# Spreading the experts' combination over the first attention units, splitting the mask matmuls, and moving one inverse root to GpSimd

## What is computed

```python
x = x + global_latent_attn(rmsnorm(x, norm1_w), ...)   # causal, 16 heads of 8, 4 key/value heads
x = x + local_gqa_attn(rmsnorm(x, norm2_w), ...)       # window of 32 keys
...
expert_inputs = jnp.einsum('bnd,bnec->becd', token_inputs, dispatch)
h = jax.nn.gelu(jnp.einsum('becd,edh->bech', expert_inputs, W1))
expert_outputs = jnp.einsum('bech,ehd->becd', h, W2)
output = jnp.einsum('becd,bnec->bnd', expert_outputs, combine)
...
x = x + attn(xn) + ffn(xn)
```

## Time and profile before

| | us |
|---|---|
| median of 3 runs | 802.06 |
| lowest and highest | 799.94, 804.38 |
| the profiled execution | 804.5 |
| its span in the trace | 802.7 |
| experts of layer 1, first `up` to last `e_out` | 555.0 to 589.3 |
| combination on PE | 589.4 to 598.5 |
| attention, first mask matmul to the end | 599.4 to 802.7 |

### The profile page before, as it was taken

How to read it: one execution, slowest core, us unless ns; L and a number is a source line. 1 busy time by engine, 2 the same in 40 slices (tenths; PEclk the granted TensorE clock), 3 DMA queues, 4 the chain that set the end, 5 groups by cost and what they waited for, 6 DMA issues and landing times.

```text
span 802.7 us, 13340 instructions
## 1 busy us (share of the span) xinstructions
PE 676.3 (84%) x4403; PEld 491.5 (61%) x4403; DVE 586.0 (73%) x863; ACT 535.1 (67%) x1021; POOL 416.6 (52%) x362
## 2 busy tenths in 40 slices
PE   5899968888988887988969876698888888888986
PEld 3588837666676675865857666687673343444433
DVE  7435679999989999899989897983435435655532
ACT  4364577868768686787787885735637657766563
POOL 6301078998989989889998897730000000000000
PEclk8799999999899997999979978899999999999998
DMA  5324558577595785755858768800200000000000
GB/s 168 106 80 132 162 159 214 169 203 208 182 243 165 174 236 176 205 185 168 233 166 203 193 178 229 249 1 27 79 2 0 1 1 2 1 2 1 14 14 27
DMA packets 80963, 99.54 MB, mean 124 GB/s; under 512 B 32496, under 2 KB 37624, under 8 KB 80896
## 3 DMA queue, kind: packets, MB, share of 16 engines
q1 hardware_dynamic: 80896, 98.70, 43.4%
HBM read 96.05 MB, written 2.72 MB: 123 GB/s over the span
## 4 chain that ended last, share of the span: by engine, by line
PE 42%; DVE 17%; ACT 15%; issue 14%; POOL 8%; DMA 3%; DVEq 0%; POOLq 0%; SPq 0%; ACTq 0%
POOL drive L648 5%; DVE ps L1161 4%; PE ps L1772 4%; PE ps L2064 3%; DVE moe L1161 3%; PE ps L1823 3%; PE ps L1838 3%; POOL hc L656 3%; PE ps L2033 3%; ACT ps L851 2%; PE ps L2041 2%; PE ps L1907 2%; PE ps L1702 2%; DVE hc L1169 2%; PE ps L2071 2%
## 5 line engine op out<-in xcount | busy, mean ns | idle before, releaser
L648 POOL TENSOR_TENSOR drive<-dtu,b_sb 128x512 f32<-128x512 f32 x160 | 202.6, 1274 | 6.0 <-DMA b_sb<-bc_rows 5.9
L656 POOL TENSOR_TENSOR hc<-moe,c_sb 128x512 f32<-128x512 f32 x128 | 162.9, 1273 | 26.6 <-DVE moe L1161 26.5
L1161 DVE TENSOR_TENSOR_SCAN moe<-ps,drive 128x512 f32<-128x512 f32 x128 | 153.5, 1199 | 0.2 <-POOL hc L656 0.2
L1772 PE MATMUL ps<-ident,hc 128*128 128x128 f32 x1024 | 147.5, 293 | 0.6 <-POOL hc L656 0.6
L1772 PEld LDWEIGHTS ps<-ident,hc 128*128 128x128 f32 x1024 | 129.8, 153 | 25.8 <-issue 24.8
L1161 DVE TENSOR_TENSOR_SCAN ps<-decay_sb,ps 128x512 f32<-128x512 f32 x96 | 117.3, 1222 | 29.0 <-ACT ps L851 14.4
L1068 ACT ACTIVATE probs<-ps 128x1024 f32<-128x1024 f32 (+1 forms) x96 | 87.6, 914 | 67.4 <-PE ps L2041 57.0
L851 ACT ACTIVATE ps<-dt,negA 128x510 f32<-128x510 f32 x160 | 105.7, 676 | 14.9 <-DVE moe L1161 11.0
L661 POOL TENSOR_TENSOR stat<-stat,halfc 128x4 f32<-128x4 f32 x7 | 7.0, 1007 | 193.4 <-DVE stat L1426 193.4
L1169 DVE TENSOR_TENSOR hc<-ps,c_sb 128x512 f32<-128x512 f32 x128 | 85.3, 666 | 0.0
L1750 PE MATMUL ps<-xm,dtuT 128*128 128x128 f32 x384 | 59.6, 305 | 14.8 <-DMA xm<-spot_rows 8.4
(11 more groups left out here) (281 smaller groups left out, 1231.0 us busy)
## 6 DMA issues: line engine op xcount, KB each, us to landing
b_sb<-bc_rows SPq DMA_DIRECT2D x128, 256.0 KB, 4.1
c_sb<-bc_rows SPq DMA_DIRECT2D x128, 256.0 KB, 4.5
xm<-spot_rows SPq DMA_DIRECT2D x48, 256.0 KB, 3.8
wbuf<-in_pack SPq DMA_DIRECT2D x16, 514.0 KB, 3.4
wbuf<-in_pack SPq DMA_DIRECT2D x8, 512.0 KB, 3.5
x_sb<-in_x SPq DMA_DIRECT2D x4, 256.0 KB, 3.6
spot_rows<-c_sb SPq DMA_DIRECT2D x4, 256.0 KB, 4.6
out<-x_sb SPq DMA_DIRECT2D x4, 256.0 KB, 2.3
```

The lines of the kernel that those rows point to most:

```text
L648: pool.tensor_tensor(drive_of(N, half), dtu[:, N // STATES % 2, half], b_sb[:, N % B_RING], ALU.mult) \
L656: pool.tensor_tensor(hc[:, 2 * (N % DEEP) + half], h_of(q), c_sb[:, N % C_RING], ALU.mult).then_inc(sem["hc_pooled"], 1)
L1161: dve.tensor_tensor_scan(h_of(q)[:, turn], decay_bank(q)[:, turn], source[:, turn], 0.0, ALU.mult, ALU.add).then_inc(sem["scan_done"], 1)
L1772: last = pe.matmul(ps[:, Y_BANK + half, block], hc[:, 2 * (N % DEEP) + half, block], ident[:], start=False, stop=True, is_transpose=True, ...
```

## The change

- The combination becomes eight events through `PREP_BANK`: `et` k (four transposes and ACT's copy to `eo`) and `cb` k (eight matmuls, and four DVE instructions that multiply by the gate and add into `x_sb`). They sit in slots 5, 6, 16, 17 (`et`) and 7, 8, 18, 20 (`cb`). The separate stage after the experts is gone.
- The events of group 1 go one slot later (`T` three), `L1` now follows unit 0.
- In the readers' list T, L, O1 and `et` now stand ahead of the slot's exponentials.
- `FILL_AT` is written out: K0 and `sqr0` with expert 1, `inv0` with 5, `split0` and turn(0,0) with 6, `rms1`, turn(0,1) and turn(0,2) with 7.
- The inverse root of group 0 is one GpSimd power of 128x80 instead of Ln and Exp on ACT.
- Each mask matmul becomes two of 64x64, so that the two heads of a unit use four different quarters of the array; two halves of the masks are loaded a second time, swapped, by two more DMAs.
- The first two `average` wait for the last expert's `e_out`.

PE's list after begins `unit0 T1 L1 unit1 Q1 unit2 turn1,0 unit3 average0 copy0 turn1,1 K1 unit4 sqr1 et0 unit5 average1 back0 turn1,2 inv1 et1 unit6 split1 rms2 cb0 unit7 average2 copy1 cb1 unit8 turn2,0 unit9 ...`, and later has `... et2 unit16 inv2 et3 unit17 average7 back4 turn3,2 split2 cb2 unit18 O10 rms3 unit19 average8 copy5 cb3 unit20 turn4,0 O20 unit21 ...`. The readers' list has `... et1 unit6 back0 inv1 unit7 average2 split1 rms2 cb0 unit8 copy1 cb1 turn2,0 unit9 ...`.

```diff
@@ -238,16 +238,19 @@
             if name != "L" or G < GROUPS // 2:
-                put(12 * G + at, name, G)
+                put(12 * G + at + (G == 1 and name not in ("rms", "O1", "O2")) + 2 * ((name, G) == ("T", 1)), name, G)
+    for k, (turned_at, added_at) in enumerate(((5, 7), (6, 8), (16, 18), (17, 20))):
+        put(turned_at, "et", k)
+        put(added_at, "cb", k)
     order, readers = [], []
...
             unit.append(("average", at // 2 - 1))
-        first = [ev for ev in here if ev[0] == "turn"]
+        first = [ev for ev in here if ev[0] in ("turn", "T", "L", "O1", "et")]
         order += here + unit
-        readers += first + unit + [ev for ev in here if ev[0] != "turn"]
+        readers += first + unit + [ev for ev in here if ev not in first]
     return order, readers
@@ -256,16 +259,18 @@
 BLOCKS = ((0, 0), (1, 1), (0, 1))
+HALF_ROWS = (slice(0, P // 2), slice(P // 2, P))
 UNITS1 = 2 * SEQS * len(BLOCKS) * KV // 2
...
 FILL = AT_READERS[:AT_READERS.index(("unit", 0))]
-assert set(FILL) == set(AT_ORDER[:len(FILL)])
-AT_ORDER, AT_READERS = AT_ORDER[len(FILL):], AT_READERS[len(FILL):]
-LATER = FILL[4:]
-FILL_AT = {e: LATER[2 * (e - 1):2 * e if e < EXPERTS - 1 else None] for e in range(1, EXPERTS)}
+EARLY_AT = AT_ORDER[:AT_ORDER.index(("unit", 0))]
+AT_ORDER, AT_READERS = AT_ORDER[len(EARLY_AT):], AT_READERS[len(FILL):]
+FILL_AT = {1: [("K", 0), ("sqr", 0)], 2: [], 3: [], 4: [], 5: [("inv", 0)], 6: [("split", 0), ("turn", 0, 0)],
+           7: [("rms", 1), ("turn", 0, 1), ("turn", 0, 2)]}
+FILL = FILL[:4] + [ev for e in range(1, EXPERTS) for ev in FILL_AT[e]]
 TURN = {ev: n for n, ev in enumerate(ev for ev in FILL + AT_ORDER if ev[0] == "turn")}
-PREP = {ev: n for n, ev in enumerate(ev for ev in FILL + AT_ORDER if ev[0] in ("T", "L", "Q", "K", "O1", "O2"))}
+PREP = {ev: n for n, ev in enumerate(ev for ev in FILL + AT_ORDER if ev[0] in ("T", "L", "Q", "K", "O1", "O2", "et", "cb"))}
 
@@ -418,7 +423,7 @@
         rope_k = sb("rope_k", [P, 2, 2, GT * KV * HD])
-        masks = sb("masks", [P, 3, P], F16)
+        masks = sb("masks", [P, 5, P], F16)
         ident16 = sb("ident16", [P, P], F16)
@@ -572,7 +577,9 @@
                                   (w_kvu, "w_kvu"), (w_kv, "w_kv"), (w_o, "w_o"), (w_g, "w_g"), (tri, "tri")):
-                    sp.dma_start(dst[:], a[name]).then_inc(sem["l1_weights_loaded"], 16)
+                    sp.dma_start(masks[:, 0:3] if name == "masks" else dst[:], a[name]).then_inc(sem["l1_weights_loaded"], 16)
+                for rows, other in (HALF_ROWS, HALF_ROWS[::-1]):
+                    sp.dma_start(masks[rows, 3:5], a["masks"][other, 0:2]).then_inc(sem["l1_weights_loaded"], 16)
                 sp.dma_start(iota32[:], a["iota32"].partition_broadcast(P)).then_inc(sem["l1_weights_loaded"], 16)
@@ -744,6 +751,10 @@
                     rms_pow(ev[1])
+                elif ev == ("sqr", 0):
+                    pool.wait_ge(sem["qk_var"], 1)
+                    pool.tensor_tensor(norm[:, 3], norm[:, 1], halfc[:, 0:1].broadcast_to([P, QH + KH]), ALU.pow) \
+                        .then_inc(sem["qk_inv"], 1)
 
@@ -991,10 +1002,10 @@
                     act.activation(qk_sqr[:], qk[:, r].rearrange("p h d -> p (h d)"), ACT.Square).then_inc(sem["qk_sq"], 1)
-                elif kind == "inv":
+                elif kind == "inv" and G:
                     act.wait_ge(sem["qk_var"], G + 1)
                     act.activation(norm[:, 2], norm[:, 1], ACT.Ln).then_inc(sem["qk_ln"], 1)
-                    act.wait_ge(sem["qk_ln"], G + 1)
+                    act.wait_ge(sem["qk_ln"], G)
                     after(act, "qk_normed", G)
@@ -1005,6 +1016,11 @@
                         .then_inc(sem["qk_hi"], 1)
+                elif kind == "et":
+                    act.wait_ge(sem["prep_ready"], PREP[ev] + 1)
+                    act.wait_ge(sem["d_turned"], 8)
+                    act.activation(eo[:, 2 * G:2 * G + 2].rearrange("p b s d -> p (b s d)"), ps[:, PREP_BANK], ACT.Copy) \
+                        .then_inc(sem["prep_free"], 1)
                 elif kind == "O1":
@@ -1050,12 +1066,6 @@
 
-            for k in range(4):
-                act.wait_ge(sem["e_turn"], k + 1)
-                act.wait_ge(sem["d_turned"], 8)
-                act.activation(eo[:, 2 * k:2 * k + 2].rearrange("p b s d -> p (b s d)"), ps[:, k], ACT.Copy) \
-                    .then_inc(sem["e_turned"], 1)
-
             def exps(U):
@@ -1387,7 +1397,7 @@
                 n = ts.stop - ts.start
-                dve.wait_ge(sem["l1_weights_loaded"], 13 * 16)
+                dve.wait_ge(sem["l1_weights_loaded"], 15 * 16)
                 link(dve.tensor_scalar(route[:, 2, ts], route[:, 0, ts], 0.0, None, ALU.is_equal))
@@ -1513,7 +1523,7 @@
                     dve.wait_ge(sem["qk_sum"], G + 1)
-                    after(dve, "qk_ln", G)
+                    after(dve, "qk_ln", G - 1)
                     dve.tensor_scalar(norm[:, 1], norm[:, 0], 1.0 / HD, RMS_EPS, ALU.mult, ALU.add).then_inc(sem["qk_var"], 1)
@@ -1525,6 +1535,13 @@
                                       ALU.subtract).then_inc(sem["qk_split"], 1)
+                elif kind == "cb":
+                    dve.wait_ge(sem["prep_ready"], PREP[ev] + 1)
+                    for t in range(4):
+                        row = x_sb[:, 4 * G + t]
+                        last = dve.scalar_tensor_tensor(row, ps[:, PREP_BANK, t * D:(t + 1) * D], rstat[:, 3, 4 * G + t:4 * G + t + 1],
+                                                        row, ALU.mult, ALU.add)
+                    last.then_inc(sem["prep_free"], 1)
                 elif kind == "O2":
@@ -1571,15 +1588,6 @@
                 fill(e + 1)
-            for k in range(4):
-                dve.wait_ge(sem["e_comb"], k + 1)
-                rows = slice(4 * k, 4 * k + 4)
-                dve.tensor_tensor(sq[:, rows], ps[:, 4 + k % 2].rearrange("p (t d) -> p t d", d=D),
-                                  rstat[:, 3, rows].unsqueeze(2).broadcast_to([P, 4, D]), ALU.mult) \
-                    .then_inc(sem["e_added"], 1)
-            dve.wait_ge(sem["e_added"], 4)
-            dve.tensor_tensor(x_sb[:], x_sb[:], sq[:], ALU.add).then_inc(sem["x1_ready"], 1)
-
             def head_out(n):
@@ -1637,7 +1645,7 @@
 
-                pe.wait_ge(sem["l1_weights_loaded"], 13 * 16)
+                pe.wait_ge(sem["l1_weights_loaded"], 15 * 16)
                 if part == 0:
@@ -1892,7 +1900,17 @@
                     pe.wait_ge(sem["heads_done"], GT * (G + 1))
-                if kind == "L":
+                if kind == "et":
+                    pe.wait_ge(sem["e_out"], EXPERTS)
+                    for n in range(4):
+                        last = pe.transpose(bank[:, n * P:(n + 1) * P],
+                                            xe[:, 2 * G + n // 2, 4 * (n % 2):4 * (n % 2) + 4].rearrange("p e c -> p (e c)"), ident[:])
+                elif kind == "cb":
+                    for t in range(4):
+                        for two in range(2):
+                            last = pe.matmul(bank[:, t * D:(t + 1) * D], slotT[:, two, 4 * G + t], eo[:, 2 * G + t // 2, two],
+                                             start=(two == 0), stop=(two == 1))
+                elif kind == "L":
                     last = pe.matmul(ps[0:LAT, PREP_BANK], w_kvd[:], xmT[:, k * GT * P:(k + 1) * GT * P], start=True, stop=True)
@@ -2000,20 +2018,6 @@
             down(EXPERTS - 1)
-            pe.wait_ge(sem["e_out"], EXPERTS)
-            for k in range(4):
-                for n, (b, s) in enumerate(((2 * k, 0), (2 * k, 1), (2 * k + 1, 0), (2 * k + 1, 1))):
-                    last = pe.transpose(ps[:, k, n * P:(n + 1) * P], xe[:, b, 4 * s:4 * s + 4].rearrange("p e c -> p (e c)"), ident[:])
-                last.then_inc(sem["e_turn"], 1)
-            for k in range(4):
-                pe.wait_ge(sem["e_turned"], k + 1)
-                after(pe, "e_added", k - 1)
-                for t in range(4):
-                    for s in range(2):
-                        last = pe.matmul(ps[:, 4 + k % 2, t * D:(t + 1) * D], slotT[:, s, 4 * k + t], eo[:, 2 * k + t // 2, s],
-                                         start=(s == 0), stop=(s == 1))
-                last.then_inc(sem["e_comb"], 1)
-
             def scores(U):
@@ -2030,8 +2034,11 @@
                     elif kt == qt:
-                        pe.matmul(ps[:, kv], ident16[:], masks[:, l].unsqueeze(1).broadcast_to([P, GROUP, P]),
-                                  start=True, stop=False)
+                        for rows in HALF_ROWS:
+                            keys = rows if kv == kvs[0] else HALF_ROWS[rows is HALF_ROWS[0]]
+                            pe.matmul(ps[keys, kv], ident16[rows, rows],
+                                      masks[rows, l if kv == kvs[0] else 3 + l].unsqueeze(1).broadcast_to([P // 2, GROUP, P]),
+                                      start=True, stop=False)
                 for kv in kvs:
@@ -2051,6 +2058,8 @@
```

(6 more changed lines are left out.)

## The result

The changed kernel takes 811.7 us (810.8 to 819.5, four runs) against 801.5 for the kernel before (799.9 to 804.4), a ratio of 1.0145 with an interval of 1.0076 to 1.0214.

What follows compares the result with a forecast made beforehand. PE was taken to lead in the attention, with ACT and DVE working round it. Terms of -7.4, +18.2, -6.3 and +2.4 (clock) gave +6.9 on the profiled 804.5, so 808.9 us at the median; range 796 to 821.

Steps and rivals of the forecast that it cites:

- Units 0 to 21: Attention's first units: moved work, masks, new waits and smaller waits together cost +18.2 us, without the clock.
- the two waits: Behind units 7 and 18: PE waits 7.0 us before cb1 and 5.4 before O10 for DVE to empty banks.
- To unit 0: From the experts to unit 0: combination, L1 and T1 leave, a wait comes; -7.4 us, without the clock.
- The new wait at turn(0,2): Among the experts: turn(0,2) waits for turn(0,1)'s copy behind rms1, so the last expert and unit 0 come 3.5 us later.
- the kept wait at turn(0,0): Among the experts: PE waits 3.5 us behind GpSimd's 13.0 us root, where it waited 3.8; gain 0.3.
- The masks: Attention: quarters work at once, saving 0.21 us per masked unit; -3.4 in units 0 to 21, -6.5 later.
- The clock: Three new waits of over 3 us each bring slow clock, 0.8 us apiece; +2.4 us.
- The copies: Units 22 to 95: Q3's wait goes, -1.6 us; T's copy holds up the exponentials, +1.8.
- The loads: SP's queue: two more loads delay the state loads behind them by 0 to 1.1 us, taken as 0.
- D: Rival, first inverse root: GpSimd's power is short, near 2.3 us; 803.8 us at the median; chance 0.20.
- B: Rival, masks: the quarters don't work together; 818.8 us with two and two, 828.6 with three passes; chance 0.17.
- C: Rival, units 7 and 18: inserted waits add under 4 us in place of 11.9; 795.9 us at the median; chance 0.18.

Runs made afterwards that it cites:

- cb_first: The changed kernel with cb ahead of all else of its slot in the readers' list; median 801.4 us, ratio 1.0008 to the kernel before.
- full_masks: The changed kernel with the mask matmuls as they were, two of 128x128 in place of four of 64x64; ratio 1.0141 to the kernel before.
- quarters_only: The kernel before with only the masks in quarters and their two extra loads; ratio 1.0034 to the kernel before.
- loads_only: The kernel before with the two extra mask loads and the wider tile, masks multiplied as before; ratio 1.0018 to the kernel before.

## Why the prediction came out, point by point

**Units 0 to 21.** The mechanism of the two waits was right in every link: which DVE operation holds which bank, in what order, and for how long (7.0 and 5.4 forecast, 6.6 and 5.0 measured; cb_first removes them and 10 us with them). With O20's 0.9 in place of 1.9 and the 2.4 for the split gone, PE's waits there rose by 10.1 of the 11.9 forecast. The stretch as a whole was under-sized: +22.5 came for 19.8, in the main because the masks saved 1.3 and not 3.4, and because 17 us of slow clock fell here, not the 1.6 us of time that two waits at 0.8 allow.

**To unit 0.** -7.8 for -6.6. The new wait at turn(0,2) and the kept wait at turn(0,0) were 3.6 and 3.1. The slow clock is 3.4 us in both kernels, so the added 0.8 was not due.

**The masks** are the term that was mis-sized most. 0.54 to 0.34 for a step was right (0.21 forecast), and it was the path that failed: shares of a chain, 31 of 48 and 16 of 16, counted as savings. -9.9 was forecast; at equal clock the traces show about -5.3 (-4.0 and -1.3), and with their clocks as they were -3.0 (changed against full_masks) and -2.8 (quarters_only against before). The timed runs show no gain at all.

**The clock.** From the first expert matmul to the end the changed kernel has 38 us at 1.2 GHz and the kernel before 23. At 0.4 each that is 6 us, an estimate, where +2.4 was forecast for three waits.

**The copies** were mis-sized the other way, +0.2 for about -2 in the later units. And the earlier trace rows has three waits for `latT`: the prediction's terms name Q1's and Q3's, not Q2's, whose 1.6 went in units 10 to 18. **The loads** were set at 0; the stretch ahead of the experts is 2.9 longer in the trace of loads_only, for reasons only partly found.

So the total came out near because errors of opposite sign met, and that part is luck: nearly 5 us too much saving from the masks, 3 to 4 too little for the clock and up to 3 left out ahead of the experts, against 2 to 3 too little from the copies, 2 too much for the waits and under 1 at the start. These are estimates, and with them some 3 us of the +7.6 in the traces stay unassigned. 6.9 was forecast, 10.2 is the difference of the medians. The rivals: D is out (the power took 13.1 us), B is out (the step is 0.34), and C is out, since the waits added 10.1 us and not under 4.

## What to carry to other kernels

When work is inserted into an in-order list through a shared bank, follow the emptying engine's list, not only the writer's: the writer waits for everything that stands ahead of the emptying. Work that is moved on one engine, from a place where it is the bottleneck to another where it is, need not save anything: here 9.1 us moved and the sum stayed at 241.2. A share of the critical chain is no measure of a saving: here 9.9 us by share were about 5 by equal stretches. And of two terms of opposite sign each wants its own run.

## What the runs showed of the hardware

GpSimd's power on 128 partitions took 1007 ns for 4 columns, 2267 for 12 and 13.11 us for 80, near one line. Four 64x64 matmuls of 512 columns on four quarters of the array took 0.41 us together, two of them writing one bank on different partitions. The time at 1.2 GHz differs between executions of identical instructions (from the first expert matmul on, 23 us in the trace of the kernel before and 8 in that of loads_only), and in the later units of the attention each us of it cost 0.4 us. Two more loads of 64 partitions, on the queue that also loads a running stage, went with 8.7 us of GpSimd's waits for that stage's rows, where the kernel before has 5.7; about 3 us more in all ahead of the experts, of which their place on the queue explains only a part.
